# Banded attention: 192 of 256 keys for each half of the queries, in 64x64 tiles of the matrix engine

## The reference

```
x = hidden_states                                # (8, 1024, 256)
xn = layernorm(x)
out = x + taylor_attention(xn) + transformer(xn)

transformer, two layers on 8 sequences of 1024 tokens:
  h = shift_token(x); q, k, v = split(h @ wqkv)  # 8 heads of 64
  q, k = rotary(l2norm(q) * qs), rotary(l2norm(k) * ks)
  a window of 128 queries sees its own 128 keys and the 128 before:
  sim = q @ k.T                                  # 128 x 256
  sim = -max where i < j, or i > j + 128, or before the sequence
  x = x + softmax(sim) @ v @ wo
  h = layernorm(shift_token(x)); a, g = split(h @ w1 + b1)
  x = x + (a * gelu(g)) @ w2 + b2
```

## Time and profile before

| | |
|---|---|
| median of 3 runs | 4146.42 us (4145.9 to 4151.79) |
| span of the profiled execution, first to last instruction | 4149.4 us |
| the profiled execution's own time | only its span is given; that lies 3.0 us above the median and within the range of the 3 runs |
| PE busy | 3919.5 us, 94% |
| PEld / DVE / ACT / POOL busy | 64% / 71% / 69% / 32% |
| mean granted TensorE clock | 0.981 of 2.4 GHz |
| DMA | 148.51 MB, 36 GB/s on average |

### The profile page before, as it was taken

How to read it: one execution, slowest core, us unless ns; L and a number is a source line. 1 busy time by engine, 2 the same in 40 slices (tenths; PEclk the granted TensorE clock), 3 DMA queues, 4 the chain that set the end, 5 groups by cost and what they waited for, 6 DMA issues and landing times.

```text
span 4149.4 us, 85963 instructions
## 1 busy us (share of the span) xinstructions
PE 3919.5 (94%) x27616; PEld 2676.0 (64%) x27616; DVE 2934.5 (71%) x8672; ACT 2873.9 (69%) x6204; POOL 1308.0 (32%) x1319
## 2 busy tenths in 40 slices
PE   7898889989959999999999999999999999999998
PEld 3444443444337777777777777777777777777776
DVE  5666676667547777777777777777777777777775
ACT  5677668767737776777777676767777676767674
POOL 2211121212023333433333333334333333333332
PEclk9999999999979999999999999999999999999999
DMA  2100110010020111011111111110111111110100
GB/s 74 33 22 13 33 33 23 12 32 22 2 108 33 44 34 40 33 43 36 38 38 38 38 36 41 35 40 33 43 37 36 38 38 38 36 43 33 40 28 16
DMA packets 130974, 148.51 MB, mean 36 GB/s; under 512 B 23664, under 2 KB 97648, under 8 KB 129904
## 3 DMA queue, kind: packets, MB, share of 16 engines
q1 hardware_dynamic: 130672, 145.19, 10.4%
HBM read 45.78 MB, written 25.17 MB: 17 GB/s over the span
## 4 chain that ended last, share of the span: by engine, by line
PE 49%; DVE 15%; issue 7%; DVEq 1%; POOL 0%; DMA 0%; ACT 0%; SPq 0%; POOLq 0%
PE f_ps L1411 9%; PE f_ps L1322 9%; PE f_ps L1396 7%; PE f_ps L1365 6%; PE f_ps L1342 5%; PE f_ps L1373 5%; DVE pr L1077 4%; DVE pr L1093 4%; PE f_ps L1327 3%; PE f_ps L1353 3%; DVE cosine L1044 2%; PE f_ps L1402 1%; DVE ssq L1052 1%; DVE act_u L1139 1%; PE f_ps L1380 1%
## 5 line engine op out<-in xcount | busy, mean ns | idle before, releaser
L1242 ACT ACTIVATE pr<-pr,nmax,rnorm 128x256 f32<-128x256 f32 x1024 | 600.5, 588 | 413.0 <-DVE nmax L1083 413.0
L1322 PE MATMUL f_ps<-wqkv_s,hT 128*128 128x512 f32 x1536 | 730.6, 612 | 11.6 <-ACT hT L1204 6.0
L495 ACT ACTIVATE weights<-t_ps,four_s 128x1024 f32<-128x1024 f32 (+3 forms) x768 | 630.8, 906 | 108.4 <-PE t_ps L600 104.6
L1396 PEld LDWEIGHTS f_ps<-hnT,w_s 128*128 128x128 f32 x5120 | 593.8, 193 | 61.5 <-issue 60.3
L1396 PE MATMUL f_ps<-hnT,w_s 128*128 128x128 f32 x5120 | 595.2, 276 | 0.8 <-DVE hnT L1129 0.8
L971 POOL TENSOR_TENSOR rstd<-ve,f_mhalf 128x1 f32<-128x1 f32 x128 | 89.9, 702 | 1371.1 <-DVE ve L1117 1371.1
L1093 DVE TENSOR_SCALAR pr<-pr,rsum 128x256 f32<-128x256 f32 x1024 | 486.3, 536 | 9.0
L1322 PEld LDWEIGHTS f_ps<-wqkv_s,hT 128*128 128x128 f32 x1536 | 272.6, 190 | 326.5 <-issue 310.1
L1077 DVE CUSTOM_DVE_ANT_0 pr<-f_ps,mask 128x256 f32<-128x256 f32 x1024 | 393.9, 422 | 111.6 <-PE f_ps L1342 78.6
L983 POOL TENSOR_TENSOR turned<-qk,rot 128x256 f32<-128x256 f32 x512 | 417.9, 837 | 49.8 <-ACT qk L1209 32.6
L1411 PE MATMUL f_ps<-w_s,act_u 128*128 128x256 f32 (+1 forms) x1536 | 389.5, 395 | 40.2 <-DVE act_u L1139 37.5
(11 more groups left out here) (126 smaller groups left out, 7193.2 us busy)
## 6 DMA issues: line engine op xcount, KB each, us to landing
kT<-kT SPq DMA_DIRECT2D x124, 256.0 KB, 2.4
vw<-vw SPq DMA_DIRECT2D x124, 256.0 KB, 2.3
xs<-x_dram SPq DMA_DIRECT2D x8, 1024.0 KB, 7.7
xn_dram<-xn SPq DMA_DIRECT2D x8, 1024.0 KB, 5.3
attn_dram<-ao SPq DMA_DIRECT2D x8, 1024.0 KB, 6.0
xin<-xn_dram SPq DMA_DIRECT2D x64, 128.0 KB, 2.0
xres<-x_dram SPq DMA_DIRECT2D x64, 128.0 KB, 2.1
xres<-attn_dram SPq DMA_DIRECT2D x64, 128.0 KB, 2.1
```

What stands on the lines that cost most here:

```text
L495: a.activation(weights[:, 2 * (u % UNITS):2 * (u % UNITS) + 2, c:512], ps[:, unit_bank(n):unit_bank(n) + 2, c:512], ACT.Square, bias=four_ ...
L1242: last = a.activation(pr[:, h, :], pr[:, h, :], ACT.Exp, bias=nmax[:, h:h + 1], scale=rnorm[:, h:h + 1], accum_out=psum[:, h:h + 1])
L1322: last = mm(ps[:, b, :], rows, wqkv_s[:, l, c, i * INNER:(i + 1) * INNER], start=(c == 0), stop=(c == KC - 1))
L1396: last = mm(ps[:, UP[j // 2], o:o + P], w1_s[:, l, c, half, j * P:j * P + P], hnT[:, c, :], start=(c == 0), stop=(c == KC - 1))
```

## The change

The queries of a window are taken in two halves of 64. For the first half only keys 0 to 191 of the 256 can be admitted, for the second only 64 to 255. Keys 64 to 191 are common to both: the middle. The 64 others are the corner, another one for each half. So each row has 192 scores (BAND). In PSUM and in `pr` two heads share 512 (384) columns so that the corners of two heads lie side by side and can be transposed together.

- `scores`: for each head four matmuls instead of one: two of 64 queries by 128 keys (middle) and two of 64 queries by 64 keys (corner), each on 64 rows and 64 columns of the array.
- `mask_scores`, `exps`, `normalise`: 192 columns for each head instead of 256, by `chances(h)`.
- `prob_T`: 12 transposes instead of 16, and `copy_pT` 3 copies instead of 4.
- `attend`: for each head one matmul over the middle (128 rows, 64 columns, 128 queries), and two over the corners (64 rows, 64 columns, 64 queries) that add to it. All middles come first, then all corners. The result lies in two banks.
- The values are held in four blocks (MIDDLE, OWN, OLDEST, NEWEST). A new `place_v` issues two DMAs in each slot, and `keep_v` three instead of one. `keep_k` moves four blocks per partition with one DMA.
- PSUM banks are dealt out anew; `gate` is gone, gelu writes into `act_u` in place; the rotary table is loaded twice straight into `rot`; `vw` is twice as wide and is cleared by POOL at the start.

```diff
+HALF = P // 2
+BAND = P + HALF
...
-        SCORES = (0, 2, 1, 3)
-        XT, HNT, K, V, Q, KT, QT, OT, WO, DOWN = 1, 3, 4, 5, 5, 4, 5, 7, 7, 6
+        SCORES = (0, 1, 2, 3)
+        XT, HNT, K, V, Q, KT, QT, OT, WO, DOWN = 2, 3, 4, 5, 5, 4, 5, 0, 7, 6
...
-        kT = per_thread("kT", [P, 2, HEADS // 2, P])
-        vw = per_thread("vw", [P, 2, INNER])
+        kT = per_thread("kT", [P, HEADS // 2, 2 * P])
+        vw = per_thread("vw", [P, 4, INNER])
...
+        def chances(h):
+            k = h // 2 % 2
+            return pr[:, h // 4 * 2 + h % 2, k * BAND:k * BAND + BAND]
...
-                sp.dma_start(kT[s][l][:, 0, :, :], kT[s][l][:, 1, :, :]).then_inc(k_kept[s][l], 16)
+                sp.dma_start(kT[s][l][:, :, 0:P], kT[s][l][:, :, P:2 * P]).then_inc(k_kept[s][l], 16)
...
-                sp.dma_start(vw[s][l][:, 0, :], vw[s][l][:, 1, :]).then_inc(v_kept[s][l], 16)
+                sp.dma_start(vw[s][l][0:HALF, MIDDLE, :], vw[s][l][HALF:P, OWN, :]).then_inc(v_kept[s][l], 16)
+                sp.dma_start(vw[s][l][0:HALF, OLDEST, :], vw[s][l][0:HALF, OWN, :]).then_inc(v_kept[s][l], 16)
+                sp.dma_start(vw[s][l][HALF:P, OLDEST, :], vw[s][l][0:HALF, OWN, :]).then_inc(v_kept[s][l], 16)
+
+            def place_v(step):
+                n, s, l, it = step
+                sp.wait_ge(v_ready, n + 1)
+                sp.dma_start(vw[s][l][HALF:P, MIDDLE, :], vw[s][l][0:HALF, OWN, :]).then_inc(v_placed[s][l], 16)
+                sp.dma_start(vw[s][l][0:HALF, NEWEST, :], vw[s][l][HALF:P, OWN, :]).then_inc(v_placed[s][l], 16)
...
+                if cur:
+                    place_v(cur)
...
-                    last = v.tensor_tensor_reduce(out=pr[:, h, :], in0=ps[:, SCORES[p], k * 256:k * 256 + 256], in1=mask[s][l][:, 0:2 * P],
+                    last = v.tensor_tensor_reduce(out=chances(h), in0=ps[:, SCORES[p], k * 256:k * 256 + BAND],
+                                                  in1=mask[s][l][:, HALF - k * HALF:HALF - k * HALF + BAND],
...
-                    last = v.tensor_scalar_mul(pr[:, h, :], pr[:, h, :], rsum[:, h:h + 1])
+                    last = v.tensor_scalar_mul(chances(h), chances(h), rsum[:, h:h + 1])
...
-                    act.wait_ge(v_kept[s][l], 16 * it)
+                    act.wait_ge(v_kept[s][l], 48 * it)
...
-                    last = a.activation(pr[:, h, :], pr[:, h, :], ACT.Exp, bias=nmax[:, h:h + 1], scale=rnorm[:, h:h + 1],
+                    last = a.activation(chances(h), chances(h), ACT.Exp, bias=nmax[:, h:h + 1], scale=rnorm[:, h:h + 1],
...
-                for i in range(4):
-                    act.wait_ge(pT_ps, 4 * n + i + 1)
+                for i in range(3):
+                    act.wait_ge(pT_ps, 3 * n + i + 1)
...
-                a.activation(oT[:, :, :].rearrange("p a n -> p (a n)"), ps[:, OT, :], ACT.Copy).then_inc(oT_ready, 1)
+                a.activation(oT[:, :, :].rearrange("p (z y) n -> p y z n", y=2),
+                             ps[:, OT:OT + 2, 0:2 * P].rearrange("p y (z n) -> p y z n", n=P), ACT.Copy).then_inc(oT_ready, 1)
...
+                if p != 1:
+                    pe.sem_inc(passed_pe, 1)
                 for k, h in enumerate(PAIRS_OF_HEADS[p]):
                     r = slice(h % 2 * HD, h % 2 * HD + HD)
-                    last = mm(ps[:, SCORES[p], k * 256:k * 256 + 256], qT[r, h // 2, :], kT[s][l][r, :, h // 2, :], start=True, stop=True)
+                    keys = kT[s][l][r, h // 2, :]
+                    middle, corner = k * 256 + k * HALF, k * 256 + (1 - k) * P
+                    for half in range(2):
+                        rows = slice(half * HALF, half * HALF + HALF)
+                        mm(ps[rows, SCORES[p], middle:middle + P], qT[r, h // 2, rows], keys[:, HALF:HALF + P], start=True, stop=True)
+                    for half in range(2):
+                        rows = slice(half * HALF, half * HALF + HALF)
+                        last = mm(ps[rows, SCORES[p], corner:corner + HALF], qT[r, h // 2, rows], keys[:, half * BAND:half * BAND + HALF],
+                                  start=True, stop=True)
...
+                    last = tr(ps[:, h // 4, (h % 4) * P:(h % 4 + 1) * P], pr[:, h // 4 * 2 + h % 2, h // 2 % 2 * 2 * P:h // 2 % 2 * 2 * P + P], id_s[:, :])
+                    if h % 4 == 3:
+                        last.then_inc(pT_ps, 1)
+                for p in range(HEADS // 2):
+                    last = tr(ps[:, 2, p * P:(p + 1) * P], pr[:, p, P:2 * P], id_s[:, :])
+                last.then_inc(pT_ps, 1)
+
+            def attend(step):
+                n, s, l, it = step
+                pe.wait_ge(v_ready, n + 1)
+                pe.wait_ge(v_placed[s][l], 32 * it + 32)
+
+                def place_of(h):
+                    return slice(h % 2 * HD, h % 2 * HD + HD), OT + h // 2 % 2, h // 4 * P
+
+                for h in range(HEADS):
+                    if h in (0, 2):
+                        pe.wait_ge(pT_ready, 3 * n + h // 2 + 1)
+                    part, bank, c = place_of(h)
+                    mm(ps[part, bank, c:c + P], vw[s][l][:, MIDDLE, h * HD:(h + 1) * HD], pT[:, h, :], start=(h < 4), stop=False,
+                       skip_group_check=True)
+                pe.wait_ge(pT_ready, 3 * n + 3)
+                pe.sem_inc(passed_pe, 1)
+                for four in range(2):
                     for half in range(2):
-                        i = 2 * h + half
-                        last = tr(ps[:, i // 4, (i % 4) * P:(i % 4 + 1) * P], pr[:, h, half * P:(half + 1) * P], id_s[:, :])
-                    if h % 2:
-                        last.then_inc(pT_ps, 1)
-
-            def attend(step):
-                n, s, l, it = step
-                pe.wait_ge(v_ready, n + 1)
-                for i in range(HEADS // 2):
-                    pe.wait_ge(pT_ready, 4 * n + i + 1)
-                    for half in range(2):
-                        for k in range(2):
-                            h = 2 * i + k
-                            last = mm(ps[k * HD:(k + 1) * HD, OT, i * P:(i + 1) * P], vw[s][l][:, half, h * HD:(h + 1) * HD],
-                                      pT[:, 2 * h + half, :], start=(half == 0), stop=(half == 1))
+                        for k in range(4):
+                            h = 4 * four + (0, 2, 1, 3)[k]
+                            part, bank, c = place_of(h)
+                            r = slice(h // 2 % 2 * HALF, h // 2 % 2 * HALF + HALF)
+                            vals = OLDEST if half == 0 else NEWEST if h // 2 % 2 == 0 else OWN
+                            last = mm(ps[part, bank, c + half * HALF:c + half * HALF + HALF], vw[s][l][r, vals, h * HD:(h + 1) * HD],
+                                      pT[r, HEADS + 2 * four + h % 2, half * HALF:half * HALF + HALF], start=False, stop=(half == 1),
+                                      skip_group_check=True)
                 last.then_inc(oT_ps, 1)
...
```

31 lines of the change are left out of this document (17 added, 14 removed).

## The result

The changed kernel takes 4197.93 us (median of 4 runs, 4193.81 to 4204.89), against 4147.84 us (4 runs, 4145.90 to 4151.79) for the kernel before in the same session: ratio 1.0116, 95% interval 1.0102 to 1.0131. I had predicted 4085, faster, with a range that ended at 4170. The profiled execution's span is 4192.2 us, 42.8 more than before, at a mean granted clock of 0.961 instead of 0.981.

What follows compares the result with a forecast made beforehand. TensorE was taken as the bound, tied with VectorE up to `down`. Four slots fall from 91.2 to 89.1 us, -59 over 28 iterations; slots outside the loop -5, start +3: -61, so 4085 us; range 3990 to 4170.

Steps and rivals of the forecast that it cites:

- the sum for the four slots: Loop iteration: 3 x 22.12 + 0.1 + 22.64 = 89.1 us instead of 91.2, -2.1 us, times 28 iterations -59.
- VectorE's late turn: add_attention starts 2.7 us late where VectorE's loop turns; VectorE stays the bound in that slot, 23.77 to 22.64 us.
- the floor: Rival, chance 0.12: issue sets small instructions' pace, 0.054 us per load with matmul in scores and attend; +2.2 us a slot, 4365 us.
- TensorE sees only some six instructions ahead: In scores, the next pair starts only beside the last corners of the one before; stage 2.57 us, +0.53.
- my stages: TensorE per slot: prob_T -0.44, scores +0.53, attend -0.20, together -0.11 us; a TensorE-only slot goes from 22.23 to 22.12.
- Masking at 355 ns: VectorE's masking with 64 columns fewer: 0.067 us saved each, 0.53 us for eight.
- Scaling: VectorE's scaling on fewer columns: 0.4 us saved for eight, bounds 0.05 and 0.9.
- The wait at `down`: TensorE's wait for VectorE's gated products: gone in three slots of four, still about 0.5 us in the fourth.
- Four tiles at a time: Rival, chance 0.20: row halves overlap in scores despite longer pairs; TensorE -1.25 us, VectorE bounds all slots, 4000 us.
- The values' DMAs: place_v and keep_v: extra DMA issues fit SyncE's idle time, at no cost that shows.
- Row halves that never overlap: Rival, chance 0.14: no row-half overlap in scores or attend's corners; TensorE +0.55 us a slot, 4163 us.
- the sum's own 0.45 us for entering the stages: Allowances in the floor rival's stage times: 0.15 us in scores and 0.3 us in attend.

Runs made afterwards that it cites:

- e2: Changed kernel with TensorE's 112 loop slots written out as straight code, other engines keeping their loops: 4035.70 us, ratio 0.9727.
- e5: Kernel before with 128 already met waits per slot spread through TensorE's program, a body of 1827 instructions: 4497.38 us, ratio 1.0843.
- e6: Changed kernel with one 192-key matmul per head in scores instead of four (result differs), a body of 1435 instructions: 4008.44 us, ratio 0.9666.
- e13: e12 with the head of TensorE's loop at instruction 0 of a 16 KB block: 4079.54 us, ratio 0.9828.
- e17: e12 with the head of TensorE's loop at instruction 230 of a block: 4214.15 us, ratio 1.0158.
- e12: Changed kernel with scores' middles as whole 128-query matmuls ahead of all corners, a body of 1687 instructions: 4190.67 us, ratio 1.0104.
- e8: Changed kernel with the loops of TensorE and VectorE both written out: 4002.32 us, ratio 0.9646.
- e9: Kernel before with the loops of TensorE and VectorE both written out: 4083.01 us, ratio 0.9855.
- e15: e13 with VectorE's 112 slots written out and TensorE's loop kept: 4020.92 us, ratio 0.9693.
- e3: Changed kernel with the values' DMAs cut to about the old bytes (two a slot instead of five; result differs): 4168.38 us, ratio 1.0053.
- e7: e2 with the scores matmuls of two pairs issued in turn, so lower and upper row loads alternate: 4025.17 us, ratio 0.9704.
- e10: e7 with VectorE's loop written out as well as TensorE's: 3993.48 us, ratio 0.9627.
- e4: Kernel before with 120 already met waits per TensorE slot, in two lumps of 60, a body of 1555 instructions: 4249.51 us, ratio 1.0246.
- e11: Changed kernel with the head of TensorE's loop at the start of a 16 KB block: 4064.48 us, ratio 0.9810.
- e18: e11 with the head of TensorE's loop at instruction 32 of a block: 4062.98 us, ratio 0.9794.

## Why the prediction was wrong

**The step that failed** is the sum for the four slots: "0.1 (the third slot's surplus over 22.46, kept)". That is all it grants TensorE at the turn of its loop. I had seen VectorE's late turn and kept it, and counted TensorE's new instructions as issue pace (the floor), never as length of the body. The turn cost 6.7 us an iteration instead of nothing. Shown by e2 (gone without the turn), e5 (back with code alone), e6 (gone with fewer instructions) and e13 against e17 (the head's place alone). In the net the stop costs less than 27 x 6.74 = 182 us, since VectorE's own turn lies beside it: 162 us, changed kernel less e2.

The rest of the sum wasn't right either. Without the stop e2 takes 4036 us, 49 under my 4085 and below even the forecast's own range of 4060 to 4115: three slots of an iteration take 21.5 to 21.7 us where I had 22.1, for `scores` gained and didn't lose. So the forecast missed by two steps of opposite sign, of which the stop is by far the larger.

The Trainium skill, "Runtime: NRT & Kernel Launch", section Instruction fetch mechanics, has the rule that I should have weighed: TensorE's instruction memory holds 2048 instructions, it is a FIFO filled in blocks of 256, and a taken branch whose target isn't in the current window of two blocks waits for a fetch. The packets of 16 KB and the stop at the branch agree. The size of 2048 agrees only roughly: e12, whose sum is 1880, was fetched anew in all 27 turns, and some turns were from 1819 on. The window of two blocks, 512 instructions, doesn't agree for TensorE: a body of 1687 turns without a packet (e13).

**The bill.** The changed kernel less the kernel before is 4197.9 - 4147.8 = +50.1 us. Without TensorE's and VectorE's turns (e8 less e9) it is -80.7. So the turns account for +130.8: they cost the changed kernel 195.6 (162.2 with TensorE's written out, 33.4 more with VectorE's) and the kernel before 64.8, which I take for VectorE's turn, since a TensorE loop that fits costs nothing that shows (e15).

**TensorE's stages.** `prob_T` 1.75 to 1.31: -0.44, as predicted. `attend` 1.90 to 1.65: -0.25, predicted -0.20. `scores` 2.03 to 2.00: -0.03, predicted +0.53, within the bounds. The reason that I gave for it, that TensorE sees only some six instructions ahead, failed: it goes ahead with 10 unissued; how far it sees, no run tells. A slot of TensorE alone went from 22.23 to 21.52; my stages sum to 22.12, and those measured to 22.23 - 0.72 = 21.51.

**VectorE.** Masking at 355 ns, as predicted. Groups of DVE, 1400 to 4000 us, beside the earlier trace rows:

```profile
L1111 DVE TENSOR_SCALAR pr<-pr,rsum 128x192 f32<-128x192 f32 x896 | 406.5, 514 | 7.9
L1094 DVE CUSTOM_DVE_ANT_0 pr<-f_ps,mask 128x192 f32<-128x192 f32 x896 | 284.9, 355 | 179.7 <-PE f_ps L1370 146.8
```

Scaling went from 542 to 514 ns in the mean, 0.22 us for eight: I took 0.4, within the bounds of 0.05 and 0.9. The wait at `down` went in three slots of four, as forecast, and here in the fourth too, as the stop gives VectorE time. Without the stop (e2) the first slot is 22.90, where I had 22.64.

**What I costed at nothing.** The values' DMAs: 29.6 us (e3), hidden only in part; some 11 of them (27 x 0.4) are longer stands at the stop. It is the one other sizeable term that I had at 0.

**The rivals.** Four tiles at a time: true in part, and in full once the rows alternate (e7), with VectorE as the next bound, as the rival said; 4000 us was its price, and e8 and e10 take 4002 and 3993, though only with both loops written out. Row halves that never overlap: fell. The floor: fell; the 32 corners of `attend` with their 32 loads take 0.62 us in the chain of waits, 19 ns for each load with its matmul, where 44 would have decided the sign (40, if the sum's own 0.45 us for entering the stages are counted, which I had left out there). I ended on the wrong side with a rival on the slow side that wasn't the right one.

**Open.** Why the edge lies where it does, why it isn't sharp, and why e4 stopped twice with a sum of 1794. VectorE's turn looks like the same mechanism, on a smaller scale: the other queue of kind "instruction" shows it in the kernel before already, there and then with VectorE's slots written out (e8):

```profile
q14 instruction: 198, 1.62, 0.1%
```

```profile
q14 instruction: 123, 1.01, 0.1%
```

75 packets of 8 KB more with the loop than without it, and between two of VectorE's branches the trace of before has 5 of them, each time but one. No run varied the length or the place of VectorE's body, so this is a reading and not shown.

## What to carry to other kernels

Count the instructions of each engine's loop body before and after a change, and look for the queue of kind "instruction" in the profile: packets in proportion to the iterations mean that the turns fetch their code, and the branch's duration says whether they wait for it. Many small matmuls in place of one large can be cheap on the array and dear in the loop. Then write the loop out, shorten the body or place its head: e11, one line more than the changed kernel, takes 4064 us, and e10 3993.

## What the runs showed of the hardware

- A loop of TensorE turned in 0.2 us where its body, counted from the start of the 16 KB block of its head, was up to 1815 instructions long (but for 2 of 27 turns at 1794, e4), and in 3.7 us, with 9 packets of 16 KB, in some turns from 1819 on and in all from 1880 on (e11, e12, e17).
- A second stand of 2.6 us comes where the head's block has few instructions left (21 in the changed kernel), none where it has 256 (e11). TensorE's idle time at a stop goes from 4.4 to 2.1 us with it. Behind all 27 stops of the changed kernel the clock falls to 1.2 GHz for a part of what follows, behind 4 of 14 in e18.
- The place of a loop's head alone made 135 us of difference (e13 and e17, the latter in 2 runs), 3.3%.
- Straight code of 300 packets ran without one wait for its code (e2).
- In the net a stop cost 162/27 = 6.0 us in the changed kernel. In e18, with the head near the start of its block, 14 stops go with 27 us more than e2, 2 us for each.
- Four 64x64 tiles ran at once (e7), at 19 ns for each load with its matmul in the corners of `attend`.
- A wait that is already met isn't free for TensorE: 120 of them (60 instructions) made a slot 0.9 us longer (e4), 128 spread out 1.7 to 2.0 (e5).
